# When the next layer's weights are loaded: chunks 1, 8 and 12 in place of 1, 5 and 9, and 9 and 11 in place of 7 and 9 for the feed-forward

## The reference

```python
qkv = shift_tokens(x) @ Wqkv[i]                     # 128 x 3072
q, k = l2norm(q) * q_scale, l2norm(k) * k_scale     # 16 heads of 64
q, k = rotary(q), rotary(k)
out = local_attention(q, k, v)                      # windows of 32, own and previous
x = out @ Wo[i] + x                                 # 1024 x 128
xn = layer_norm(shift_tokens(x))
a, gate = split(xn @ W1[i] + b1[i])                 # 128 x 682
x = (a * gelu(gate)) @ W2[i] + b2[i] + x            # 341 x 128
```

## Time and profile before

| what | value |
|---|---|
| three runs | 3610.72, 3613.35 and 3627.78 us; median 3613.35 us |
| the profiled execution | 3621.26 us |
| its span in the profile | 3619.1 us |
| its mean granted clock of TensorE | 0.969 |
| PE, DVE, ACT, POOL busy | 92%, 77%, 69%, 75% of the span |

### The profile page before, as it was taken

The page is one execution under the profiler, slowest core; times in us unless marked ns, Lnnn a source line. Parts: engine busy times, 40 slices in busy tenths (PEclk is TensorE's granted clock), DMA queues, the critical chain, the costliest instruction groups (busy, mean ns, idle before and its releaser), DMA issues. The chain is left out here.

```text
span 3619.1 us, 152088 instructions
## 1 busy us (share of the span) xinstructions
PE 3322.5 (92%) x64040; PEld 2535.6 (70%) x64040; DVE 2800.4 (77%) x4983; ACT 2482.6 (69%) x3080; POOL 2720.1 (75%) x2152
## 2 busy tenths in 40 slices
PE   6899999999999999998677899999999999999996
PEld 4777777777777777776335777777777777777774
DVE  5778878788878878876447788778888878878883
ACT  4677777777767777775225677777777777777773
POOL 5888888788878878875007888888888888888881
PEclk8999999999999999999889999999999999999998
DMA  3333333333333333332002333333333333333320
GB/s 96 77 83 82 80 83 82 78 86 79 79 84 78 80 87 77 81 88 64 6 0 67 79 85 82 80 84 78 83 86 78 81 83 80 81 83 77 78 74 25
DMA packets 208997, 272.66 MB, mean 75 GB/s; under 512 B 55748, under 2 KB 103744, under 8 KB 208320
## 3 DMA queue, kind: packets, MB, share of 16 engines
q1 hardware_dynamic: 208320, 262.94, 28.2%
HBM read 60.35 MB, written 1.05 MB: 17 GB/s over the span
## 5 line engine op out<-in xcount | busy, mean ns | idle before, releaser
L1240 POOL TENSOR_TENSOR V<-RAWQK,TAB 128x512 f32<-128x512 f32 x768 | 953.2, 1275 | 443.5 <-PE PS L340 434.3
L388 PE MATMUL PS<-WH,XH 128*128 128x512 f32 x1152 | 518.4, 450 | 99.9 <-ACT VS L770 86.3
L770 ACT ACTIVATE VS<-PS 128x1024 f32<-128x1024 f32 x192 | 196.5, 1023 | 481.0 <-PE PS L390 357.2
L1282 POOL TENSOR_TENSOR V<-V,U 128x1024 f32<-128x1024 f32 x192 | 455.6, 2373 | 14.9
L390 PE MATMUL PS<-WL,XH 128*128 128x512 f32 x1152 | 465.5, 404 | 0.0
L389 PE MATMUL PS<-WH,XL 128*128 128x512 f32 x1152 | 464.5, 403 | 0.0
L1266 POOL TENSOR_TENSOR V<-V,U 128x1024 f32<-128x1024 f32 x192 | 457.5, 2383 | 0.0
L1275 POOL TENSOR_TENSOR V<-V,RN 128x1024 f32<-128x1024 f32 x192 | 372.2, 1938 | 93.7 <-DVE RN L918 92.1
L340 PEld LDWEIGHTS PS<-EYE,V 128*128 128x128 f32 x3072 | 348.2, 141 | 110.2 <-issue 99.0
L510 PEld LDWEIGHTS PS<-OT,WO 128*128 128x128 f32 x3072 | 373.6, 192 | 21.4 <-issue 5.1
L340 PE MATMUL PS<-EYE,V 128*128 128x128 f32 x3072 | 371.3, 274 | 10.3 <-ACT OT L777 5.1
(11 more groups left out here) (162 smaller groups left out, 7100.0 us busy)
## 6 DMA issues: line engine op xcount, KB each, us to landing
V<-VS SPq DMA_DIRECT2D x3072, 64.0 KB
ROTB<-c_rot SPq DMA_DIRECT2D x192, 128.0 KB, 2.5
WSTAGE<-wqkv SPq DMA_DIRECT2D x33, 512.0 KB
WO<-wo SPq DMA_DIRECT2D x12, 512.0 KB, 3.8
W<-w SPq DMA_DIRECT2D x12, 341.0 KB, 3.1
QKS<-qks SPq DMA_DIRECT2D x12, 128.0 KB, 3.7
W<-w SPq DMA_DIRECT2D x12, 114.0 KB
RAWQK<-x SPq DMA_DIRECT2D x4, 256.0 KB, 3.7
```

Of the source, the lines that this page charges most:

```text
L388: pe.matmul(o, XH[:, p, :], WH[:, w, cols], start=True, stop=False)
L1240: ins = pool.tensor_tensor(paired(V[:, k])[:, :, :, h * half:(h + 1) * half], split(RAWQK[:, k])[:, :, :, (1 - h) * half:(2 - h) * half], ...
L1282: pool.tensor_tensor(V[:, 1], V[:, 1], U[:, 1], ALU.add).then_inc(k_turned, 1)
```

## The change

The numbers of the chunks after which SyncE issues a weight load become constants. The second and third thirds of Wqkv go from i = 5 and 9 to i = 8 and 12, W1 goes from i = 7 to 9, and W2 from i = 9 to 11, where it comes behind `load_attn`. The first third stays at i = 1 and `load_attn` at i = 11. The waits ahead of the loads, the steps in which ScalarE and GpSimd round and split a third, and all other instructions stay as they are.

```diff
+WQKV_AT, W1_AT, W2_AT, ATTN_AT = (1, 8, 12), 9, 11, 11
...
                     w, i = layer_of(inv, c), c % CH
-                    if i in (1, 5, 9) and w + 1 < 2 * DEPTH:
-                        k = i // 4
+                    if i in WQKV_AT and w + 1 < 2 * DEPTH:
+                        k = WQKV_AT.index(i)
                         l = (w + 1) % DEPTH
                         sp.wait_ge(w_split, 3 * (w + 1) + k)
                         sp.dma_start(WIN_[:, :], a["wqkv"][l:l + 1, :, k * HEADS * DH:(k + 1) * HEADS * DH].rearrange(
                             "l p n -> p (l n)")).then_inc(w_in, 16)
-                    if i == 11 and w + 1 < 2 * DEPTH:
+                    if i == ATTN_AT and w + 1 < 2 * DEPTH:
                         held(projected, inv * NCH + c // CH * CH)
                         held(xa_done, xa_count(inv, c // CH * NG - 1))
                         load_attn(w + 1)
-                    if c >= CH and i == LAG:
+                    if c >= CH and i == W1_AT:
                         for h in hid:
                             sp.wait_ge(h, 2 * (inv * NGR + c // CH * NG))
                         load_w1(w)
-                    if c >= CH and i == LAG + 2:
+                    if c >= CH and i == W2_AT:
                         sp.wait_ge(y_done, inv * NGR + c // CH * NG)
                         load_w2(w)
```

## The result

The changed kernel takes 3507.93 us (median of 4 runs, 3505.96 to 3509.7), the kernel before 3612.03 us (3607.09 to 3627.78) in the same comparison: 104.1 us faster, a ratio of 0.9708 with a 95% interval of 0.9685 to 0.9732. The profiled execution took 3509.7 us, 111.6 us less than the profiled one of before. The forecast was 3507.2 us.

What follows compares the result with a forecast made beforehand. The prediction took PE at 2.4 GHz as the bound wherever undisturbed. A gain of 114.0 us less 7.8 for two moved loads, 106.2, took the median of 3613.35 to 3507.2 us; range 3490 to 3540.

Steps and rivals of the forecast that it cites:

- What bounds the kernel, and where it loses: PE bounds the undisturbed last layer, 247.2 us for slots 0 to 14; the other eleven layers lose 113.0 us.
- The excess of the slots: Slots 6-7 and 10-11 over eleven layers exceed the last layer's by 44.8 and 69.2 us; this 114.0 us goes.
- The bounds of 86.3 and 123.8: Limits on the 114.0 us: PE's waits for ScalarE's values copy below, ScalarE's waits for a landing before it above.
- The price of the two loads at their new places: Wqkv's second and third thirds, now in slots 8 and 12, cost 2 x 3.9 = 7.8 us over eleven layers.
- The sum: Whole kernel: 114.0 - 7.8 = 106.2 us gained, from the median of 3613.35 to 3507.2 us.
- W1 and W2: Loads moved to the ends of chunks 9 and 11: nothing gained and nothing lost, cost 0 each.
- The margin of W1: W1, loaded behind chunk 9, lands 7.1 us before PE first reads it, with 3.1 us to landing.
- Rival B: At chunks 9 and 13, window copies can't proceed before the load lands: 34.1 us cost, 3533.5 us; chance 0.08.
- Rival C: Long slots come from the rounding and splitting themselves, so nothing moves: 3613 us; chance 0.05.
- Rival D: At the new places each load's whole landing falls on the path: 22 x 6.0 = 132 us, 3631 us; chance 0.03.

Runs made afterwards that it cites:

- small loads: Changed kernel, but only 64 of 1024 columns of Wqkv's second and last thirds loaded (32 KB in place of 512 KB): 3501.5 us, ratio 0.9692 to the kernel before.

## Why the prediction was right

**What bounds the kernel, and where it loses.** Right. Taking the last layer as the undisturbed one gave both the place and the size of the loss, and the changed kernel's layers now match it.

**The excess of the slots, 114.0 us.** Right, 116.9 measured (48.3 and 68.6 against 44.8 and 69.2). It is 2.9 us more because layers 0 and 6 have less to do in slots 6-7 than the last layer (30.2 and 29.9 us in the changed kernel, against 33.2), so their excess was more than a comparison with it shows. The bounds of 86.3 and 123.8 held too. The prediction read the fall of the clock at one stop; it came behind 16 of the 22.

**The price of the two loads at their new places, 7.8 us.** No run shows this term. The small loads put it at 0.7 us, with an interval that holds 7.8 as well. Slots 8-9 and 12-14 grew by 3.5 and 1.0 us over the kernel before, whose rows are these:

```profile
sum 357.71, PE 351.83 PEld 279.46 DVE 305.21 ACT 265.09 POOL 323.05; mean PE 31.98 PEld 25.41 DVE 27.75 ACT 24.10 POOL 29.37
sum 542.92, PE 535.69 PEld 419.61 DVE 453.42 ACT 416.04 POOL 480.02; mean PE 48.70 PEld 38.15 DVE 41.22 ACT 37.82 POOL 43.64
```

Slots 0-5, where nothing changed, shrank meanwhile from 1087.8 to 1084.8. So the 3.9 us from which I took the price are of the size of the scatter, and the term was most likely too large.

**The sum.** 106.2 us forecast; 111.6 between the two profiled executions and 104.1 between the medians. The sum was made against a profiled execution that lay 7.9 us over its median, so part of the closeness to the median (0.7 us) is luck. Without the term for the loads the forecast would have been 3499.4: nearer for the profiled pair, 8.6 us off for the medians.

**W1 and W2.** Right, 0 each: with the waits gone, their old places do as well as the new ones, and moving them alone changes no time. What the prediction did not see is that W1's new place would be too late without the other half of the change. The margin of W1, 7.1 us, was real: in the changed kernel 9.6 to 11.7 us lie between the issue of its load and PE's first read, and 3.1 of them are the landing. One chunk later costs everything, with a stall 1.4 us shorter than worked out. W2's place left a small trace: at slot 12 the issue of the first copy took 1.1 to 1.7 us in four of eleven layers, where it was 0.52 in all of them before, and ScalarE waited for a landing behind it in three; the slot is 0.1 us longer on average.

**Rival B** (the loads get in the way) was wrong for the changed kernel, and its mechanism was not seen in the one before either. I had put the whole excess down to the late issue of the copies, and that stands; but the wait is only about 82 us of it. Some 29 us are there only when loads stand between the wait and the late copies, and what the rows show of them is time on SyncE's queue (the issues of the loads, and at slot 10 the long issue of the first copy, whose cause stays open) and the clock that falls behind the longer stops. This did not touch the sum, which was read at the end of the chain, where all of it arrives together. A forecast made up from 4.8 us of delay less about 3 us of slack, 22 times, some 40 us, would have come out far too small. The rule of the Trainium skill that was set beside this rival (DMA: Bandwidth & Descriptors, section Queues, rings and completion order) has two halves: descriptors are consumed in ring order, and data descriptors carry no barrier. These runs can't tell what either does here: the last copy is issued some 12 us after the load and the load lands 4.2 us after its issue (median), so copies that were held until then would still have landed in time. No run shows the rings themselves.

**Rival C** fell: every rounding and splitting is still there, and the time is gone. **Rival D** fell with the changed kernel, whose slots 8-9 and 12-14 grew by 4.5 us in all and not by 132, and again with the run that puts the load directly ahead of the copies.

## What to carry to other kernels

A wait in a DMA queue costs what stands behind it, not what it guards: give a load with a wait the first place at which its wait is surely met, and take as the last place the one from which it still lands before its reader comes. Both edges are sharp, one chunk each here (5 costs about 45 us at the second third; 6 and 10 nothing, nor 8 and 12; 9 and 13 together 34; W1 at 9 nothing, at 10 about 100). And where one layer or iteration lacks the suspect, subtract it slot by slot from the others before tracing any chain.

## What was not expected

A load costs what it takes of the queue, by the slack of what is behind it. Directly ahead of window copies that are on time, 22 loads of 512 KB cost at most a few us. In the kernel before, ahead of copies already 5 us late, the loads made up about 29 us, and about half of what they did to these slots was the clock: a stop 2 us longer met a lower clock in ten layers in place of two.

The issue of one 64 KB copy lasted 2.3 to 2.95 us, in place of 0.51, where it followed directly on a third of Wqkv and the two loads of W2 (nine cases, all at slot 10 of the kernel before). With one 512 KB load ahead, at slot 6, it was 0.51 us in ten of eleven.

A stop of PE can cost more than its idle time: 40 of the 117 us were slower work, nearly all of it behind 16 of the 22 stops, with waits for ScalarE's copy of at most 5.6 us; and 2.0 us came on top of each stop of 8.3 us.
